# Codebook levels picked already scaled, plain w_eff additions, work moved to GpSimd, no filling products

## The reference

```python
lora_delta = lora_B @ lora_A * (32 / 64)
cb = codebook / clip(max(abs(codebook)), 1e-8)           # 8 levels
scale = exp(scale_log)                                   # one per output row and group of 128 inputs
normalized = (weight + lora_delta).reshape(O, 4, 128) / scale
thresholds = (cb[:-1] + cb[1:]) * 0.5
quantized = cb[searchsorted(thresholds, normalized)]
w_eff = (quantized * scale).reshape(O, I) + lora_delta   # the straight-through form reduces to this
a = x @ w_eff.T
x = x + attention(a; Wqkv, bqkv, Wo, bo)                 # one head of 128, 128 keys
base = x @ W.T; gates = softmax over the top 2 of (x @ Wr.T + 5 at the language's expert)
moe = base + 2 * lora experts of rank 16, weighted by gates
x = x + moe @ (ffn_scale * (qweight - zero_point)).T + bias
```

## Time and profile before

| | |
|---|---|
| median of the timed runs | 108.01 us |
| lowest and highest of 3 | 108.0 and 108.59 us |
| the profiled execution, its own time | 107.76 us |
| its span, first to last instruction | 105.8 us |
| TensorE busy in it | 101.3 us, 513 matmul records |
| DVE, ACT, POOL busy | 67.9, 52.1, 31.8 us |

### The profile page before, as it was taken

How to read it: one execution, slowest core, us unless ns; L and a number is a source line. 1 busy time by engine, 2 the same in 40 slices (tenths; PEclk the granted TensorE clock), 3 DMA queues, 4 the chain that set the end, 5 groups by cost and what they waited for, 6 DMA issues and landing times.

```text
span 105.8 us, 1459 instructions
## 1 busy us (share of the span) xinstructions
PE 101.3 (96%) x513; PEld 84.1 (79%) x513; DVE 67.9 (64%) x163; ACT 52.1 (49%) x92; POOL 31.8 (30%) x40
## 2 busy tenths in 40 slices
PE   6999999999999999999999999999999999999980
PEld 6748568889788899899888786888898888888850
DVE  0199899889999999525999753014946802572441
ACT  4077898999989932934222239272037204002000
POOL 4000246799709570399000056400000400000000
PEclk9999999999999999999999999999999999999999
DMA  1999999960000000000000000000000640000083
GB/s 40 338 344 301 410 400 406 404 253 0 0 3 0 0 0 0 9 0 0 0 0 0 0 0 0 6 0 0 0 0 0 237 160 0 6 0 0 3 297 99
DMA packets 4599, 9.83 MB, mean 93 GB/s; under 512 B 752, under 2 KB 1008, under 8 KB 4592
## 3 DMA queue, kind: packets, MB, share of 16 engines
q1 hardware_dynamic: 4448, 9.48, 24.6%
q10 hardware_dynamic: 144, 0.26, 0.6%
HBM read 7.64 MB, written 2.10 MB: 92 GB/s over the span
## 4 chain that ended last, share of the span: by engine, by line
PE 89%; DMA 4%; DVE 2%; ACT 1%; DVEq 1%; issue 0%
PE psum L860 19%; PE psum L862 19%; PE psum L861 19%; PE psum L885 7%; DMA lora<-in_lora 4%; PE psum L876 3%; PE psum L895 3%; PE psum L910 3%; PE psum L901 3%; PE psum L905 3%; PE psum L1010 2%; PE psum L1031 2%; PE psum L1025 2%; ACT moe L462 1%; PE psum L1017 1%; PE psum L926 1%
## 5 line engine op out<-in xcount | busy, mean ns | idle before, releaser
L662 DVE COPY_PREDICATED cond_work<-cond_work,psum 128x1024 f32<-128x1024 int32 x10 | 13.7, 1366 | 1.1 <-ACT cond_work L363 0.7
L860 PE MATMUL psum<-G_hi,xT_hi 128*128 128x512 f32 x32 | 12.7, 398 | 0.0
L862 PE MATMUL psum<-G_hi,xT_lo 128*128 128x512 f32 x32 | 12.5, 390 | 0.0
L861 PE MATMUL psum<-G_lo,xT_hi 128*128 128x512 f32 x32 | 12.5, 390 | 0.0
L363 ACT ACTIVATE cond_work<-cond_n,cut_bias 128x1024 f32<-128x1024 f32 x10 | 11.2, 1143 | 0.6 <-DVE cond_n L699 0.6
L578 POOL TENSOR_TENSOR hl<-hl,hl_bias 128x272 f32<-128x272 f32 (+2 forms) x4 | 3.1, 774 | 26.4 <-ACT hl L374 14.4
L523 POOL TENSOR_TENSOR xT_lo<-xT,xT_hi 128x1024 fp32r<-128x1024 f32 x4 | 9.6, 2411 | 3.2 <-DVE cond_work L668 3.2
L860 PE MATMUL psum<-xT_hi,split_b_hi 128*128 128x512 f32 x24 | 9.6, 401 | 0.0
L862 PE MATMUL psum<-xT_hi,split_b_lo 128*128 128x512 f32 x24 | 9.4, 391 | 0.0
L861 PE MATMUL psum<-xT_lo,split_b_hi 128*128 128x512 f32 x24 | 9.4, 390 | 0.0
L885 PE MATMUL psum<-hlT,xT 128*128 128x136 f32 x64 | 8.4, 281 | 0.0
(11 more groups left out here) (166 smaller groups left out, 237.4 us busy)
## 6 DMA issues: line engine op xcount, KB each, us to landing
out<-cond_work SPq DMA_DIRECT2D x7, 256.0 KB, 2.1
cond_n<-in_cond_w SPq DMA_DIRECT2D x2, 512.0 KB, 6.6
xT<-in_x_t SPq DMA_DIRECT2D x2, 512.0 KB, 7.6
q_i<-in_q_t SPq DMA_DIRECT2D x4, 256.0 KB, 7.4
moe<-in_moe_w SPq DMA_DIRECT2D x4, 256.0 KB, 7.4
xT<-in_x_t SPq DMA_DIRECT2D x1, 1024.0 KB, 12.4
wqkv_n<-in_wqkv SPq DMA_DIRECT2D x1, 768.0 KB, 10.3
hlT<-in_hl_t SPq DMA_DIRECT2D x1, 272.0 KB, 5.7
```

Source lines behind the costliest of these rows:

```text
L662: dve.copy_predicated(half(level, h), beyond[n % len(beyond)].bitcast(I32), psum[EARLY][:, j + 1:j + 2].to_broadcast([P, 2 * C])).then_inc ...
L860: pe.matmul(out_ap, l_hi, r_hi, start=first, stop=False)
L861: pe.matmul(out_ap, l_hi, r_lo, start=False, stop=False)
L862: return pe.matmul(out_ap, l_lo, r_hi, start=False, stop=last)
```

## The change

1. `floor` (16 values, first level times the group's scale) is computed in the DVE's setup; the table of picks in PSUM grows from 8 values to 7 x 16 (level times scale), computed before the threshold biases.
2. POOL, not ACT, writes the first level of half 0, from `floor`; `set_level` leaves ACT. Half 1 is written from `floor` too.
3. A pick's source is 8 values (one per group), each broadcast over 128, instead of one.
4. `w_eff` is one addition of 512 elements for each block row instead of four scaled additions of 128.
5. The remainders of w_eff blocks 0 and 1 move from DVE to POOL, each put in front of a Wqkv remainder.
6. The four filling products leave TensorE.

```diff
+            pool.wait_ge(floor_ready, 1)
+            pool.tensor_copy(by_group(half(level, 0)), floor_of(0)).then_inc(level_set, 1)
             moe_rest(1)
...
-            pool.tensor_copy(half(level, 1), levels[:, 0:1].to_broadcast([P, 2 * C])).then_inc(level_late_set, 1)
+            pool.tensor_copy(by_group(half(level, 1)), floor_of(1)).then_inc(level_late_set, 1)
...
             pool.wait_ge(w_eff_ready, 2)
             x_lo(1)
+            w_eff_rest(0)
             wqkv_rest(0)
-            pool.wait_ge(w_eff_lo_ready, 2)
+            w_eff_rest(1)
             wqkv_rest(1)
             wqkv_rest(2)
             wqkv_rest(3)
-            pool.wait_ge(w_eff_lo_ready, CT)
+            pool.wait_ge(w_eff_late_lo_ready, 2)
...
-            dve.tensor_scalar(psum[EARLY][:, 0:LEVELS], cb, cb_tmp[:, 3:4], None, ALU.mult).then_inc(picks_ready, 1)
...
             dve.wait_ge(scale_ready, 1)
+            dve.tensor_scalar(floor[:, :], scale, levels[:, 0:1], None, ALU.mult).then_inc(floor_ready, 1)
             dve.reciprocal(inv_scale[:, :], scale).then_inc(inv_scale_ready, 1)
...
-                dve.copy_predicated(half(level, h), beyond[n % len(beyond)].bitcast(I32),
-                                    psum[EARLY][:, j + 1:j + 2].to_broadcast([P, 2 * C])).then_inc(picked, 1)
+                at = GROUPS * j + GROUPS // 2 * h
+                dve.copy_predicated(by_group(half(level, h)), by_group(beyond[n % len(beyond)].bitcast(I32)),
+                                    psum[EARLY][:, at:at + GROUPS // 2].unsqueeze(2).to_broadcast(
+                                        [P, GROUPS // 2, P])).then_inc(picked, 1)
...
-                for g in range(CT * o, CT * (o + 1)):
-                    ins = dve.scalar_tensor_tensor(g_block(level, g), g_block(level, g), scale[:, g:g + 1],
-                                                   g_block(delta, g), ALU.mult, ALU.add)
-                ins.then_inc(w_eff_ready, 1)
+                dve.tensor_tensor(level[:, o, :], level[:, o, :], delta[:, o, :], ALU.add).then_inc(w_eff_ready, 1)
...
+            dve.tensor_tensor(psum[EARLY][:, 0:CUTS * GROUPS].rearrange("p (j g) -> p j g", j=CUTS),
+                              levels[:, 1:LEVELS].unsqueeze(2).to_broadcast([P, CUTS, GROUPS]),
+                              scale.unsqueeze(1).to_broadcast([P, CUTS, GROUPS]), ALU.mult).then_inc(picks_ready, 1)
             dve.tensor_scalar(cut_bias[:, :], cuts[:, :], -CUT_GAIN, None, ALU.mult).then_inc(cut_bias_ready, 1)
...
             pick(3, 1)
-            w_eff_lo(0)
-            w_eff_lo(1)
             pick(4, 1)
...
-            idle_turns(FILL)
```

## The result

| | before | changed |
|---|---|---|
| median of 20 runs | 107.97 us | 108.49 us |
| lowest to highest | 107.35 to 108.84 us | 108.30 to 108.71 us |
| the profiled execution: own time, span | 107.76, 105.8 us | 108.71, 106.4 us |
| what lies around its span | 1.98 us | 2.36 us |

The ratio is 1.0053, interval 1.0034 to 1.0072: about half a percent slower, small but clear of noise. Two more things differ: the changed kernel hardly varies, and more time lies outside its span. About 0.6 us came in the span of the two profiled executions (106.35 - 105.78), 0.4 outside. They are two questions. Three executions of the kernel before that fell into a slower state (108.93, 108.96 and 109.05 us) are in the medians of the table of experiments, but not in its ratios.

The account below looks back on a forecast made before the run. The prediction took TensorE's instruction order from 4.64 us on as the bound. Fill, setup, level, picks and w_eff each came to 0 us on 107.76 us, giving a median of 108.0 us, range 107.3 to 108.9.

Parts of the forecast that it names:

- What bounds the kernel: TensorE's instruction order from 4.64 us on; edits on other engines can't shorten it, only lengthen it through a late operand.
- The setup operations: Floor and the larger table early on the DVE: 0.4 us later, at most 0.51, hidden by cover, so 0.
- The picks: 14 predicated copies on the DVE with eight broadcast values: 0 more each, at most 0.82 us.
- POOL's order: POOL's remainders after x_lo(1): first wqkv remainder ready at 35.9 us, needed at 38.02, all hidden: 0.
- The clock: Rival: TensorE's clock falls in the hole the fill leaves, 1.7 us lost, 109.7 us; chance 0.06.
- The first level on POOL: POOL's copy near 6.5 us beside DVE operations: 0 to 0.32 us on the DVE, taken as 0 on the path.
- cover of 0.60: Slack of 0.60 us between the rounded q block's remainder, ready at 14.66, and TensorE's need of it at 15.26.
- POOL's copy shuts the DVE out: Rival: the copy holds two-input DVE work for 1.04 us, 0.95 us lost, 108.9; chance of 0.2 or more 0.10.
- Two of my own signs of being wrong: First logits product before 9.0 us; loads at 14.13 and 15.26 moving later than the product at 11.29 does.
- The fill: Removing TensorE's filling products, 0.89 us ending 0.11 us after x0 landed at 9.09: -0.11 to +0.09 us, taken as 0.
- turns into more cover: Plain w_eff and moved remainders gain the DVE about 2.8 us between 29 and 44 us; no TensorE wait shortened: 0.
- The sum: All edits 0 us on the profiled execution's own 107.76 us; the median is 0.25 above it, so 108.0 us.

Follow-up runs that it names:

- e9: The kernel before with only the two new DVE setup operations added, written to places that nothing reads: ratio 1.0008.
- e8: The changed kernel as it is, run again beside the kernel before: 108.48 us, ratio 1.0049.
- e14: The changed kernel with two semaphores merged away, its work and order the same: 108.48 us, ratio 1.0045 to the kernel before.
- e4: The kernel before without its four filling products, nothing else changed: 108.23 us, ratio 1.0004.
- e6: The changed kernel with floor and half 0's first level made by ACT, and the table of picks moved behind `w_full(0)`: 107.71 us, ratio 1.0002 to the kernel before.
- e2: The kernel before with POOL instead of ACT writing the first level of half 0, nothing else: 108.31 us, ratio 1.0007.
- e7: The changed kernel with POOL's first copy halved to 512 elements, ACT writing the other half: 108.26 us, ratio 1.0022 to the kernel before.
- e15: The changed kernel with 13 tiny operations added to the DVE's queue in idle time: 108.32 us, ratio 1.0010 to the kernel before.
- e17: The kernel before with w_eff as one plain addition per block row, the group's scale left out, 12 DVE operations fewer: 108.79 us, ratio 1.0061.
- e18: The kernel of e6 with 14 tiny operations added to the DVE's queue in idle time: 107.69 us, ratio 0.9977 to the kernel before.

## Why the prediction was wrong

The forecast was no change, 108.0. The change is slower by 0.34 to 0.72%, 108.49. The time lies inside the stated range and within the 1% that I called the same, but only because these were wide. The step that failed is the one on the first level, where a hold by POOL's copy was priced at nothing on the path and cost 0.85 us on the DVE; and the sum took the time around the span as fixed.

**What bounds the kernel** was right, and so was the consequence that an elementwise edit can only lengthen it, by overrunning a cover. **The setup operations** were right (0.4 us taken; 0.14 + 0.19 = 0.33 measured, e9 shows them hidden). **The picks** were right: 1.364 and 1.374 us on average, against 1.366 and 1.364 before, with eight broadcast values as with one. **POOL's order** was right to 0.6 us: the first wqkv remainder was ready at 36.5 instead of my 35.9, with no wait behind it. **The clock** didn't fall.

**The first level on POOL** is the step that failed. I had the copy's time, its length and its neighbours right, and read the remainder that took 1.01 us instead of 0.69 as a price of 0.32 us and wrote "So the price is from 0 to 0.32 us on the DVE". Even that price, with the setup's 0.4, overran the cover of 0.60 by my own sum, and I took 0. The rows say more when their ends are put side by side. POOL's subtraction ended at 15.40 + 1.31 = 16.71, the remainder began at 16.25 and ended at 17.26: it ran its last 0.55 us after POOL had finished. It had been held for what was left of POOL's instruction, and only little was left. A copy of 1.04 us that begins together with a chain of short operations holds it nearly whole. The trace of the kernel before even has a one-input operation of four elements held in this way, which the prediction doesn't use; where POOL is idle, at 77.2 us, it takes 0.17:

```profile
62.13 0.73 DVE L770 TENSOR_SCALAR neg_max<-neg_max 128x4 f32<-128x4 f32 x1
...
62.07 0.77 POOL L578 TENSOR_TENSOR hl<-hl,hl_bias 128x272 f32<-128x272 f32 x1 [12.04 <-ACT hl_bias L492]
```

The rival "POOL's copy shuts the DVE out" had that mechanism, and I gave it 0.10. Its way of reckoning holds where the covers lie: the rounded block was ready at 14.73 instead of 13.48, 1.25 us late, less its cover of 0.65 is 0.60, and TensorE's product was 0.56 late. Its lateness of 1.55 was too high: 0.85 for the hold, 0.33 for the setup operations and 0.15 for the small transfer, less 0.08 that the DVE caught up, are 1.25. The growth of the span by 0.57 us between the two profiled executions has those 0.15 us of chance in it; the medians with the early clock give 0.4 (e8: 106.1 against 105.7) to 0.5 (e14: 106.1 against 105.6).

Two of my own signs of being wrong came: the first logits product started before 9.0 us (8.41), and the loads of 14.13 and 15.26 moved by 0.71 and 0.70 us (14.84, 15.96) where the first G product moved by 0.29. The first of them cost nothing, the second is the loss.

**The fill**: no gain was right, the reason only half. The landing at 9.09 that I built on was one draw. In the profiled executions of all these kernels x0 landed 5.4 to 6.5 us after its issue. Where it comes at 8.1 the fill is no cover but path; it was free in the changed kernel because the DVE was later still.

**w_eff** "turns into more cover" was right for the changed kernel, though with less than I had added up: the last remainder ended at 43.27 us, not near 41, and TensorE began to read them at 45.56. I had missed one place where the DVE is nearly late, the expert remainder before `y_x(0)` (e4: 0.3 us given back; e6: not). It is what would have made the shorter w_eff worth something. One of its pairs also met POOL. The DVE's timeline of the changed kernel, both pairs, and POOL's beside the second:

```profile
30.55 1.26 DVE L674 TENSOR_TENSOR cond_work<-cond_work,delta 128x512 f32<-128x512 f32 x2
...
40.06 1.82 DVE L674 TENSOR_TENSOR cond_work<-cond_work,delta 128x512 f32<-128x512 f32 x2
...
37.75 2.97 POOL L521 TENSOR_TENSOR wqkv_lo<-wqkv_n,wqkv_hi 128x384 fp32r<-128x384 f32 x3
```

The second pair began at 40.06 and POOL ended at 40.72: 0.66 us were left of POOL's instruction, and the pair took 0.56 more than the first. It is the same hold at the same price, this time under cover.

**The sum** added to the profiled execution's own 107.76 us and so took the 1.98 us around the span as fixed. They became 2.30 (median of the 20 runs). That is a term which the sum didn't have. Where the clock rises early it is about 0.3 of the 0.76 us between the kernels (e8), and the span most of the rest. Why it grew is open.

**The spread.** The changed kernel varies by 0.4 us, the kernel before by 1.5. Where the clock rises late, the LoRA products and their evictions are late, and in the kernel before the DVE's addition waits for them. In the changed kernel the DVE comes to that addition at 8.59 us, later than they. In e8 and the kernel before beside it, where the mean clock was 1.000 (9 and 24 executions), the changed kernel took 108.48 and the kernel before 107.72; where it was lower (3 and 11), 108.60 and 108.55. So the change costs about 0.76 us or nearly nothing, by the moment at which the clock rises. That the evictions are what hides it there is read from the profiles, not tested.

## What to carry to other kernels

When work moves from ACT to POOL, lay its whole duration over the DVE's timeline: a DVE operation on SBUF operands that meets it can be held until it ends, and a chain of one-element operations is then as slow as the copy. Read a stretched operation by its end, not by its length: if it ends a fixed time after a neighbour's end, it was held, and the price in another place is what will be left of the neighbour there (here less 0.14 us). A landing time in one trace is one draw; before a fill or a cover is built on a margin of 0.1 us, look at more than one execution.

## What the runs showed of the hardware

- A held DVE operation cost what was left of POOL's instruction less about 0.14 us: 0.88 for 1.01 left (changed kernel), 0.72 for 0.87 (e2), 0.45 for 0.59 (e7), 0.54 for 0.66 (the w_eff pair).
- The hold also takes an operation with one SBUF tensor input and a scalar: seven elements took 0.89 us beside POOL's copy (e2), 0.17 without; four elements 0.73 and 0.17 in the kernel before.
- Operations of the DVE that read one operand from PSUM were not held in these runs. Predicated copies whose value comes from PSUM took 1.32 to 1.42 us beside POOL in all runs, 1.34 to 1.37 where POOL was idle; the subtractions of 384 elements from PSUM (L742 in the changed kernel) 0.56 us either way. Of the operations on SBUF alone, reciprocals of four elements took 0.18 us beside POOL as without it.
- The DVE's queue shorter by 12 to 14 operations went with 0.13 to 0.4 us more outside the span, in three kernels and in both directions (e15, e17, e18); between 83 and 92 semaphores made none beyond 0.05. The Trainium skill (Runtime: NRT & Kernel Launch, the launch sequence) counts a semaphore reset of a fixed number per engine after the kernel, which agrees with the latter. No trace here explains the former.
- TensorE's granted clock rose from the lower level (1.2 GHz) to the higher (2.4 GHz) at 3.9 to 7.2 us after the span's start in different executions, with the same warm-up products. Holes of 0.2 to 1.2 us in TensorE's work behind the rise never brought it back to the lower level (changed kernel: risen at 5.0, a hole of 1.2 us before 11.58).
